# A graph network kernel on Trainium2: bias of the first merge from PSUM, and roots and shifts of the norms moved ahead

## The chip, the cores and the metric

One core of a Trainium2 chip runs the whole program. The metric is device microseconds of one execution.

## What is computed

The input is a graph of N = 3125 nodes with 256 features each (x) and E = 53125 edges (src, dst, sorted by dst, with loops). Four blocks follow each other; each is added to its input and normalised by row:

```python
x = _layernorm(x + _L0_gnn_ref(x, src, dst, ...))   # attention over edges, 8 heads, then out @ Wo.T + bo
x = _layernorm(x + _L1_gnn_ref(x, ..., src, dst))   # attention with additive scores, 4 heads
x = _layernorm(x + _L2_gnn_ref(x, src, dst, ...))   # 5 GIN layers with batch norm
x = _layernorm(x + _L3_gnn_ref(x, edge_index, ...)) # 3 SAGE layers

def _layernorm(x, axis=-1, eps=1e-05):
    m = jnp.mean(x, axis=axis, keepdims=True)
    v = jnp.var(x, axis=axis, keepdims=True)
    return (x - m) / jnp.sqrt(v + eps)
```

The change touches the sum x + bo of the first block, and all four layernorms.

## The kernel before, in words

The node rows stand in SBUF as x, 128 partitions by NT = 25 tiles of 256, and are handled in NSLAB = 5 slabs of SLAB = 5 tiles. The program is a sequence of phases (`Phase`), each with a block of instructions for every engine and a barrier of all engines at its end: prepare, edges and merge of the first block, norm 0, tables, edges and merge of the second block, norm 1, the GIN layers, norm 2, the SAGE layers, norm 3. Within a phase every engine has its own queue in the order in which the code is written, and waits on semaphores.

**The merge** (`merge_parts`, called for the first block with `biased=(x, bias_out)`). Sums over parts of edge groups are combined: TensorE turns 28 tiles of rows into three PSUM banks (L1370), VectorE scales them by an inverse (`make_rows`, L1415), POOL scatters each tile to the array out0 in memory with an indirect DMA (L1522). Meanwhile VectorE runs scans over the chunks; TensorE turns their result, ScalarE copies it, and POOL scatters it in four more indirect DMAs (L1530). POOL then waits until all are stored. The PSUM bank `side_ps` is read once at the start of this phase. At the end of its queue VectorE computes index columns (L1505, L1509) and adds the output bias, loaded as `bias_out` (a row of 256, the same on all partitions), to the five slabs of x (L1514), whose rows SyncE has loaded.

**The norm** (`residual_norm`). What is added comes in one of two ways. With `by_tile` (norms 0, 2 and 3) TensorE brings a tile at a time into a PSUM bank `in_ps`: for norm 0 it turns a tile of the loaded `more` (L1767), ScalarE copies it (`copy_more`, L1723), TensorE multiplies it by the weight w_out (L1776); for norms 2 and 3 it turns a tile of h_t (L1757). VectorE adds it to x (`add_tile`, L1651). In norm 1 a whole slab is added from SBUF (`add_slab`, L1661). Then VectorE takes the statistics of each tile (L1653), closes the slab (`close_slab`: aggregate L1668, variance plus epsilon into `std`, L1670), ScalarE takes the root (`root`, L1701), VectorE the reciprocal (L1676) and the shift, minus mean times reciprocal (`make_shift`, L1678), and ScalarE normalises each tile (`normalise`, L1706). In norms 0, 1 and 2 TensorE turns the normalised tile into `out_ps` (L1796) and ScalarE copies it (`copy_turned`, L1711). In norm 0 TensorE also makes the products alpha from it (L1804), which ScalarE copies by slab (L1716), SyncE stores, and POOL gathers into `alpha_parts` (L1641) as soon as the slabs that a gather needs are stored. In norm 3 SyncE stores the rows to the output (L1613).

Three orders matter for the change. On VectorE, the `by_tile` norms make the shift of a slab only after the first AHEAD = 2 tiles of the next slab are added, and norm 1 makes it ahead of the next slab:

```python
for s in range(NSLAB):
    if s and not by_tile:
        make_shift(s - 1)
    add_slab(s)
    for t in tiles(s):
        add_tile(t)
        if s and by_tile and t % SLAB == AHEAD - 1:
            make_shift(s - 1)
    close_slab(s)
```

On ScalarE, the root of a slab is the first instruction of that slab's turn, so it stands behind the copies that end the turn of the slab before (the last turned tiles; in norm 0 also two `copy_more`). On TensorE, the turns of normalised tiles and the bringing in of tiles AHEAD of the next slab alternate in a fixed order, which the change leaves alone.

Of the kernel before, what the change touches and what calls it, by code (L numbers as in the profile page):

```python
# [9 lines left out]
ALU = mybir.AluOpType  # L10
# [1281 lines left out]
def merge_parts(nc, keep, layer, out_rows, scale, loads=(), biased=None):  # L1292
# [5 lines left out]
    with Phase(nc) as ctx:  # L1298
# [112 lines left out]
        def _(v):  # L1411
# [91 lines left out]
            if biased:  # L1503
                to, of = biased
                nc.vector.tensor_copy(base[:, :], keep["part_node"][:, :]).then_inc(base_set, 1)  # L1505
                v.wait_ge(base_set, 1)
                for g in range(NSLAB):
                    of_slab = slice(CT + g * SLAB if g else 0, CT + (g + 1) * SLAB)
                    nc.vector.tensor_scalar(keep["alpha_index"][:, of_slab], base[:, of_slab], float(-g * SLAB * P), 0.0, ALU.add,  # L1509
                                            ALU.max).then_inc(apart_set, 1)  # L1510
                v.wait_ge(fetched, 16 * len(loads))
                for s in range(NSLAB):
                    slab = slice(s * SLAB, (s + 1) * SLAB)
                    nc.vector.tensor_tensor(to[:, slab, :], to[:, slab, :], of[:, :].unsqueeze(1).to_broadcast([P, SLAB, D]), ALU.add)  # L1514

        @block.gpsimd
        def _(pool):
# [25 lines left out]
def residual_norm(nc, keep, scratch, layer, add=None, added_t=None, turned_to=None, rows_to=None,  # L1543
# [8 lines left out]
    with Phase(nc) as ctx:  # L1552
# [93 lines left out]
        def _(v):  # L1646
# [25 lines left out]
            def make_shift(s):  # L1672

                slab = span(s)
                v.wait_ge(rooted, s + 1)
                nc.vector.reciprocal(std[:, slab], std[:, slab]).then_inc(inv, 1)  # L1676
                v.wait_ge(inv, s + 1)
                nc.vector.scalar_tensor_tensor(out=shift[:, slab], in0=mean_var[:, slab, 0], scalar=-1.0, in1=std[:, slab],  # L1678
                                               op0=ALU.mult, op1=ALU.mult).then_inc(shifted, 1)

            for s in range(NSLAB):
                if s and not by_tile:
                    make_shift(s - 1)
                add_slab(s)
                for t in tiles(s):
                    add_tile(t)
                    if s and by_tile and t % SLAB == AHEAD - 1:
                        make_shift(s - 1)
                close_slab(s)
            make_shift(NSLAB - 1)  # L1690
            if wide > D:
# [5 lines left out]
        def _(act):  # L1697
# [21 lines left out]
            def copy_more(t):  # L1719
                act.wait_ge(more_turned, t + 1)  # L1720
                if t >= 2:
                    act.wait_ge(in_turned, t - 1)
                nc.scalar.activation(more_t[:, t % 2, :, :], turn_ps[t % 2][:, 0:D].rearrange("p (k n) -> p k n", k=KH),  # L1723
                                     ACT.Copy).then_inc(more_copied, 1)

            if weight is not None:
                for t in range(SLAB + AHEAD):
                    copy_more(t)
            for s in range(NSLAB):
                root(s)  # L1730
                for t in tiles(s):
                    normalise(t)
                    if turned_to is not None and t % SLAB:
                        copy_turned(t - 1)
                    if alpha_to is not None and s and t % SLAB == 1:
                        copy_alpha(s - 1)
                    if weight is not None and t + SLAB + AHEAD < NT and t % SLAB < SLAB - AHEAD:
                        copy_more(t + SLAB + AHEAD)
                if turned_to is not None:
                    copy_turned(t)  # L1740
                if weight is not None and s + 2 < NSLAB:
                    for u in range(AHEAD):
                        copy_more((s + 2) * SLAB + u)
# [854 lines left out]
```

## Time and profile before

| what | value |
|---|---|
| median of 3 runs | 3120.46 us (3116.26 to 3121.49) |
| the profiled execution, its own time | 3124.26 us |
| its span, first to last instruction | 3122.5 us |
| mean granted TensorE clock | 0.930 of full speed |
| busy: TensorE, VectorE, ScalarE, POOL | 90%, 50%, 36%, 32% |
| first merge with its bias, until the first load of norm 0 | to 761.75 us |
| norm 0, norm 1 | about 762 to 832, 1493 to 1530 us |
| norm 2, norm 3 | about 2491 to 2531, 3087 to 3122 us |

Times in the trace are microseconds from the start of the span. A timeline row shows the start, the duration, the engine, the line, the operation with its output and inputs, how many instructions were merged into the row, and in brackets how long the engine was idle before and what ended that. Instructions on VectorE and ScalarE overlap a little with the next one, so the distance between starts is shorter than a duration.

### The profile page before, as it was taken

What the parts mean: (1) busy time and instruction counts of PE and PEld (TensorE: products, weight loads), DVE (VectorE), ACT (ScalarE), POOL (GpSimd) and SP (SyncE); (2) the same over time, 40 slices, a digit from 0 to 9 for tenths busy, and PEclk for the clock granted to TensorE, in tenths of its full rate; (3) what the DMA queues carried; (4) which work ended last, traced back from release to release, by engine and by line L of the source; (5) the groups of instructions that cost most, each with busy time, mean ns of one, the idle gap of its engine ahead of it and who ended that gap; (6) DMA issues with size and microseconds to landing.
All of it is one profiled execution on the core that took longest, in us unless ns stands there. A gap on an engine that the chain in (4) does not pass through costs nothing. (4 is left out here: it accounts for less than half of the span.)

```text
span 3122.5 us, 54367 instructions
## 1 busy us (share of the span) xinstructions
PE 2812.2 (90%) x17824; PEld 2045.7 (66%) x17824; DVE 1559.0 (50%) x2731; ACT 1117.4 (36%) x3112; POOL 988.6 (32%) x1020
## 2 busy tenths in 40 slices
PE   6789999994878999996599999999999879999997
PEld 4679999983668888985255555556555455565553
DVE  8689999975277878885412315133151340120203
ACT  6135555551446777772302204031040340110102
POOL 4477777745377777763000101001010000000000
PEclk7989999995878999997699999999999989999998
DMA  6799999953248989992343341424324034233321
GB/s 232 234 316 317 316 319 317 314 197 120 43 111 140 144 153 148 157 144 59 120 156 102 110 130 53 160 78 136 129 68 132 1 134 139 84 129 129 105 96 41
DMA packets 327372, 469.35 MB, mean 150 GB/s; under 512 B 154903, under 2 KB 237927, under 8 KB 326453
## 3 DMA queue, kind: packets, MB, share of 16 engines
q1 hardware_dynamic: 264228, 285.42, 33.6%
q0 software_dynamic: 59088, 176.67, 18.7%
q10 hardware_dynamic: 3776, 3.80, 0.4%
q8 instruction: 144, 2.36, 0.3%
q14 instruction: 136, 1.11, 0.1%
HBM read 412.09 MB, written 55.44 MB: 150 GB/s over the span
## 5 line engine op out<-in xcount | busy, mean ns | idle before, releaser
L1138 ACT ACTIVATE sums<-e_part_ps 128x384 f32 x832 | 413.6, 497 | 402.3 <-PE e_part_ps L1036 287.0
L2014 PE MATMUL gin_sum_ps<-slab,high 128*128 128x391 f16 x2000 | 499.3, 331 | 1.9 <-DMA slab<-adj 1.5
L2014 PE MATMUL gin_sum_ps<-slab,low 128*128 128x391 f16 x2000 | 499.2, 331 | 0.0
L846 POOL DMA_INDIRECT e_from_src<-val,src x416 | 393.3, 946 | 157.5 <-issue 98.5
L846 POOL DMA_INDIRECT e_from_src<-vk,src x416 | 393.4, 946 | 142.5 <-issue 105.7
L2361 PE MATMUL sage_sum_ps<-slab,high 128*128 128x391 f16 x1200 | 298.6, 330 | 7.2 <-DVE low L2443 4.1
L1034 PE MATMUL e_part_ps<-e_onehot,e_from_src 128*128 128x129 f32 x1664 | 286.1, 296 | 14.4 <-ACT ends L1140 7.7
L2361 PE MATMUL sage_sum_ps<-slab,low 128*128 128x391 f16 x1200 | 298.4, 330 | 0.0
L2191 DVE SCALAR_TENSOR_TENSOR z_t<-h_t,gin_own,gin_sum_ps 128x391 f32<-128x391 f32 x80 | 44.8, 618 | 490.1 <-PE gin_sum_ps L2014 490.1
L2076 POOL TENSOR_SCALAR h_t<-h_t 128x391 f32<-128x391 f32 x32 | 40.6, 1279 | 783.3 <-DVE h_t L2221 783.3
L2014 PEld LDWEIGHTS gin_sum_ps<-slab,low 128*128 128x128 f16 x2000 | 195.5, 98 | 140.5 <-issue 3.6
L914 DVE TENSOR_TENSOR e_from_src<-e_from_src,e_fixed 128x2048 f32<-128x2048 f32 x104 | 237.5, 2284 | 87.8 <-ACT e_fixed L1119 86.4
L2014 PEld LDWEIGHTS gin_sum_ps<-slab,high 128*128 128x128 f16 x2000 | 195.3, 98 | 130.6 <-issue 4.1
L1034 PE MATMUL e_part_ps<-x,e_from_src 128*128 128x129 f32 x1664 | 268.7, 284 | 3.0 <-DVE e_from_src L914 2.3
L2085 ACT ACTIVATE gin_y_t<-gin_proj_ps,gin_columns 128x391 f32<-128x391 f32 x80 | 46.8, 585 | 572.6 <-PE gin_proj_ps L2027 572.6
L1034 PEld LDWEIGHTS e_part_ps<-e_onehot,e_from_src 128*128 128x128 f32 x1664 | 228.1, 199 | 32.1 <-ACT ends L1140 17.9
L1034 PEld LDWEIGHTS e_part_ps<-x,e_from_src 128*128 128x128 f32 x1664 | 231.0, 192 | 22.1 <-DVE e_from_src L914 4.0
L1004 PE MATMUL e_spread_ps<-e_window,x 128*128 128x256 f32 x832 | 216.1, 387 | 14.8 <-DMA e_window<-q_part 13.7
L2449 DVE TENSOR_TENSOR z_t<-sage_sum_ps,sage_inv_degree_all 128x391 f32<-128x391 f32 x48 | 24.0, 558 | 352.7 <-PE sage_sum_ps L2361 352.7
L2418 ACT ACTIVATE h_t<-sage_proj_ps,sage_columns 128x391 f32<-128x391 f32 x48 | 25.6, 584 | 412.3 <-PE sage_proj_ps L2376 412.3
L2361 PEld LDWEIGHTS sage_sum_ps<-slab,high 128*128 128x128 f16 x1200 | 116.6, 98 | 84.9 <-DVE low L2443 5.9
L2361 PEld LDWEIGHTS sage_sum_ps<-slab,low 128*128 128x128 f16 x1200 | 117.0, 98 | 83.6 <-issue 1.0
(325 smaller groups left out, 4824.7 us busy)
## 6 DMA issues: line engine op xcount, KB each, us to landing
slab<-adj SPq DMA_DIRECT2D x160, 977.5 KB, 4.8
e_window<-q_part SPq DMA_DIRECT2D x416, 128.0 KB
adj<-e_counts SPq DMA_DIRECT2D x8, 1250.0 KB
adj<-e_counts SPq DMA_DIRECT2D x8, 1193.8 KB
e_from_src<-vk,src POOLq DMA_INDIRECT x416
e_from_src<-val,src POOLq DMA_INDIRECT x416
e_window<-alpha_part SPq DMA_DIRECT2D x416, 4.0 KB
vk<-pr_kv_out SPq DMA_DIRECT2D x25, 256.0 KB, 4.1
```

Of the source, the lines that this page charges most:

```text
L846: nc.gpsimd.indirect_dma_start(from_src[:, b, j, :], None, by_src, bass.IndirectOffsetOnAxis(ap=keep["src"][:, g * G + j:g * G + j + 1], a ...
L914: nc.vector.tensor_tensor(from_src[:, b, :, 0:D].rearrange("p j (h d) -> p j h d", h=H), from_src[:, b, :, 0:D].rearrange("p j (h d) -> p ...
L1004: mm = nc.tensor.matmul(to, onehot_t[:, r, j, :], window[:, r, j, :], start=True, stop=True)
L1034: nc.tensor.matmul(part_ps[s][:, k * ENDS:(k + 1) * ENDS], from_src[:, b, j, k * P:(k + 1) * P], onehot[:, b, j, :], start=True, stop=True)
L1138: nc.scalar.activation(keep["sums"][:, :, bass.ds(starts[j], P)], of[:, :, 0:P], ACT.Copy).then_inc(whole_copied, 1)
L2014: mm = nc.tensor.matmul(sum_ps[KH * n + m][:, 0:AN], part[:, t, m * P:(m + 1) * P], slab[:, s, n, k * AN:(k + 1) * AN], start=(t == 0 and ...
L2076: nc.gpsimd.tensor_scalar(h_t[:, 1, cols(b)], h_t[:, 1, cols(b)], 0.0, None, ALU.max).then_inc(floored, 1)
L2085: nc.scalar.activation((z_t if p else y_t)[:, m, cols(b)], proj_ps[v % (2 * KH)][:, 0:AN], ACT.Identity, bias=columns[:, 3 * p, m:m + 1], ...
L2191: nc.vector.scalar_tensor_tensor(out=z_t[:, m, cols(b)], in0=h_t[:, m, cols(b)], scalar=own[:, l:l + 1], in1=sum_ps[KH * n + m][:, 0:AN], ...
L2361: mm = nc.tensor.matmul(sum_ps[KH * n + m][:, 0:AN], part[:, t, m * P:(m + 1) * P], slab[:, s, n, k * AN:(k + 1) * AN], start=(t == 0 and ...
L2418: nc.scalar.activation(h_t[:, m, cols(b)], proj_ps[v % (2 * KH)][:, 0:AN], ACT.Relu if l + 1 < LAYERS else ACT.Identity, bias=columns[:, m ...
L2449: nc.vector.tensor_tensor(z_t[:, m, cols(b)], sum_ps[KH * n + m][:, 0:AN], inv_degree[:, cols(b)], ALU.mult).then_inc(evacuated, 1)
```

## The change

The bias row is first copied to the free PSUM bank `side_ps`, and the five adds read it there. In the `by_tile` norms the shift of a slab is made ahead of the next slab's first tile, as in norm 1. On ScalarE the root of slab s + 1 is issued right after the last normalise of slab s, ahead of the copies that follow it; the root of slab 0 stands alone in front. No instruction is added except the one copy.

```diff
                 v.wait_ge(fetched, 16 * len(loads))
+                nc.vector.tensor_copy(side_ps[:, 0:D], of[:, :]).then_inc(base_set, 1)
+                v.wait_ge(base_set, 2)
                 for s in range(NSLAB):
                     slab = slice(s * SLAB, (s + 1) * SLAB)
-                    nc.vector.tensor_tensor(to[:, slab, :], to[:, slab, :], of[:, :].unsqueeze(1).to_broadcast([P, SLAB, D]), ALU.add)
+                    nc.vector.tensor_tensor(to[:, slab, :], to[:, slab, :],
+                                            side_ps[:, 0:D].unsqueeze(1).to_broadcast([P, SLAB, D]), ALU.add)
...
             for s in range(NSLAB):
-                if s and not by_tile:
+                if s:
                     make_shift(s - 1)
                 add_slab(s)
                 for t in tiles(s):
                     add_tile(t)
-                    if s and by_tile and t % SLAB == AHEAD - 1:
-                        make_shift(s - 1)
                 close_slab(s)
...
+            root(0)
             for s in range(NSLAB):
-                root(s)
                 for t in tiles(s):
                     normalise(t)
+                    if t % SLAB == SLAB - 1 and s + 1 < NSLAB:
+                        root(s + 1)
                     if turned_to is not None and t % SLAB:
                         copy_turned(t - 1)
```

How the queues read, by the program's order (lines in the changed kernel are up to 3 higher). VectorE in norm 0, from the end of one slab into the next, before:

```order
L1668 BN_AGGR n_mean_var<-n_stats 128x2 x5
L1670 TENSOR_SCALAR n_std<-n_mean_var 128x5
L1651 TENSOR_TENSOR x<-x,n_in_ps 128x256
L1653 BN_STATS n_stats<-x 128x6
L1651 TENSOR_TENSOR x<-x,n_in_ps 128x256
L1653 BN_STATS n_stats<-x 128x6
L1676 RECIPROCAL n_std<-n_std 128x5
L1678 SCALAR_TENSOR_TENSOR n_shift<-n_mean_var,n_std 128x5
L1651 TENSOR_TENSOR x<-x,n_in_ps 128x256
L1653 BN_STATS n_stats<-x 128x6
```

The same place of VectorE's queue in the changed kernel:

```order
L1671 BN_AGGR n_mean_var<-n_stats 128x2 x5
L1673 TENSOR_SCALAR n_std<-n_mean_var 128x5
L1679 RECIPROCAL n_std<-n_std 128x5
L1681 SCALAR_TENSOR_TENSOR n_shift<-n_mean_var,n_std 128x5
L1654 TENSOR_TENSOR x<-x,n_in_ps 128x256
L1656 BN_STATS n_stats<-x 128x6
L1654 TENSOR_TENSOR x<-x,n_in_ps 128x256
L1656 BN_STATS n_stats<-x 128x6
```

The reciprocal and the shift moved past two tiles, so they now directly follow the variance (n_std) on which the root between them depends. ScalarE in norm 0, from the last but one normalise of a slab to the first of the next, before:

```order
L1706 ACTIVATE x<-x,n_shift,n_std 128x256
L1711 ACTIVATE x_t<-n_out_ps 128x2x128
L1706 ACTIVATE x<-x,n_shift,n_std 128x256
L1711 ACTIVATE x_t<-n_out_ps 128x2x128 x2
L1723 ACTIVATE n_more_t<-n_turn_ps 128x256 x2
L1701 ACTIVATE n_std<-n_std 128x5
L1706 ACTIVATE x<-x,n_shift,n_std 128x256
```

The same place of ScalarE's queue in the changed kernel:

```order
L1707 ACTIVATE x<-x,n_shift,n_std 128x256
L1712 ACTIVATE x_t<-n_out_ps 128x2x128
L1707 ACTIVATE x<-x,n_shift,n_std 128x256
L1702 ACTIVATE n_std<-n_std 128x5
L1712 ACTIVATE x_t<-n_out_ps 128x2x128 x2
L1724 ACTIVATE n_more_t<-n_turn_ps 128x256 x2
L1707 ACTIVATE x<-x,n_shift,n_std 128x256
```

The root moved ahead of two copies of turned tiles and two copies of input tiles; in norms 1 and 2 the last two don't exist, and in norm 3 none of the four.

## Rows read from the trace of the kernel before

**Rows 1.** The page, busy time of the engines (us, share, instructions).
```profile
PE 2812.2 (90%) x17824; PEld 2045.7 (66%) x17824; DVE 1559.0 (50%) x2731; ACT 1117.4 (36%) x3112; POOL 988.6 (32%) x1020
```
**Rows 2.** Timeline of POOL, end of the first merge (start, duration, operation, idle before).
```profile
737.63 7.70 POOL L1522 DMA_INDIRECT out<-m_rows,part_index  x1 [0.30 <-issue]
745.64 0.98 POOL L1522 DMA_INDIRECT out<-m_rows,part_index  x1 [0.30 <-issue]
...
755.94 0.89 POOL L1530 DMA_INDIRECT out<-m_chunk_rows,chunk_index  x1 [0.30 <-issue]
```
**Rows 3.** Timeline of VectorE and SyncE, end of the first merge.
```profile
737.38 7.09 DVE L1514 TENSOR_TENSOR x<-x,bias_out 128x1280 f32<-128x1280 f32 x5
...
761.75 3.94 SPq L1607 DMA_DIRECT2D n_more<-out  x5
```
**Rows 4.** Timelines of ScalarE, VectorE and TensorE in norm 0, before slab 2.
```profile
795.98 0.39 ACT L1711 ACTIVATE x_t<-n_out_ps 128x256 f32<-128x256 f32 x1 [0.83 <-PE n_out_ps L1796]
...
797.62 0.20 ACT L1701 ACTIVATE n_std<-n_std 128x5 f32<-128x5 f32 x1
800.76 0.60 ACT L1706 ACTIVATE x<-x,n_shift,n_std 128x256 f32<-128x256 f32 x1 [2.95 <-DVE n_shift L1678]
...
796.76 0.17 DVE L1670 TENSOR_SCALAR n_std<-n_mean_var 128x5 f32<-128x5 f32 x1
798.47 0.42 DVE L1651 TENSOR_TENSOR x<-x,n_in_ps 128x256 f32<-128x256 f32 x1 [1.54 <-PE n_in_ps L1776]
...
796.41 0.61 PE L1804 MATMUL n_alpha_ps<-w_alpha,x_t 128*128 128x8 f32 x4
...
801.41 0.44 PE L1796 MATMUL n_out_ps<-ident,x 128*128 128x128 f32 x2 [1.89 <-ACT x L1706]
```
**Rows 5.** Timelines of ScalarE and VectorE in norm 2, before slab 1.
```profile
2502.93 0.39 ACT L1711 ACTIVATE h_t<-n_out_ps 128x256 f32<-128x256 f32 x1
...
2505.96 1.09 ACT L1706 ACTIVATE x<-x,n_shift,n_std 128x256 f32<-128x256 f32 x2 [1.65 <-DVE n_shift L1678]
...
2503.90 0.17 DVE L1670 TENSOR_SCALAR n_std<-n_mean_var 128x5 f32<-128x5 f32 x1
```
**Rows 6.** Timelines of VectorE and ScalarE in norm 3, slabs 3 and 4.
```profile
3106.77 0.17 DVE L1670 TENSOR_SCALAR n_std<-n_mean_var 128x5 f32<-128x5 f32 x1
3106.85 0.41 DVE L1651 TENSOR_TENSOR x<-x,n_in_ps 128x256 f32<-128x256 f32 x1
...
3111.67 0.17 DVE L1670 TENSOR_SCALAR n_std<-n_mean_var 128x5 f32<-128x5 f32 x1
3112.11 0.19 DVE L1676 RECIPROCAL n_std<-n_std 128x5 f32<-128x5 f32 x1 [0.27 <-ACT n_std L1701]
...
3112.54 2.56 ACT L1706 ACTIVATE x<-x,n_shift,n_std 128x256 f32<-128x256 f32 x5 [0.46 <-DVE n_shift L1678]
```
**Rows 7.** Groups by line and shape, VectorE (busy us, mean ns, idle before).
```profile
L852 DVE COPY e_fixed<-iota 128x128 f32<-128x128 f32 x2 | 0.6, 294 | 31.5 <-PEq L74 31.5
```
**Rows 8.** Timelines of VectorE and POOL in the first block's edge phase.
```profile
179.87 2.28 DVE L914 TENSOR_TENSOR e_from_src<-e_from_src,e_fixed 128x2048 f32<-128x2048 f32 x1
...
181.32 0.95 POOL L846 DMA_INDIRECT e_from_src<-vk,src  x1 [0.30 <-issue]
```
**Rows 9.** All instructions of line 846, first block: ns min/median/max.
```profile
L846 POOL DMA_INDIRECT e_from_src<-vk,src x416: 940/946/955, 146.3 to 666.0; - x139
```
**Rows 10.** Timeline of POOL, second merge.
```profile
1478.19 0.98 POOL L1522 DMA_INDIRECT out<-m_rows,part_index  x1 [0.30 <-issue]
```
**Rows 11.** Timelines of ScalarE (slab 0) and POOL (gathers) in norm 0.
```profile
775.95 1.28 ACT L1701 ACT_TABLE_LOAD   x1
...
819.88 0.94 POOL L1641 DMA_INDIRECT alpha_parts<-alpha,alpha_index  x1 [6.57 <-DMA alpha<-n_alpha]
```
**Rows 12.** Timeline of ScalarE in norm 1, before slab 1.
```profile
1506.92 0.20 ACT L1701 ACTIVATE n_std<-n_std 128x5 f32<-128x5 f32 x1
1507.58 1.09 ACT L1706 ACTIVATE x<-x,n_shift,n_std 128x256 f32<-128x256 f32 x2 [0.46 <-DVE n_shift L1678]
```

## The prediction

> **What bounds the kernel now.** I read the page first: TensorE is busy for 90% of the span [rows 1]. But the change touches none of the stages in which that work lies. It touches the end of the first merge and the four residual norms, short stages between barriers, so what counts is which engine ends each of them. For that I read the timeline of each engine there.
>
> First merge. POOL scatters the merged rows to memory by indirect DMAs, one every 1.29 us: from 745.64 to 755.94 there are eight such steps [rows 2]. One of them, issued at 737.63, takes 7.70 us instead of 0.98 [rows 2]. In the same time, from 737.38 to 744.47, VectorE adds the bias to x in five instructions [rows 3]. POOL resumes 0.9 us after the last of them, which is what one issue takes. ScalarE and TensorE are long done, VectorE ends at 744.47, and the next stage's first load comes at 761.75 [rows 3], 4.92 us after POOL's last issue ends (755.94 + 0.89). So POOL ends this stage and the long issue is on the path.
>
> Norms. ScalarE's first normalising instruction of a slab waits for the slab's shift. In norm 0 the variance of slab 2 is there at 796.76, and the normalise starts at 800.76, 4.00 us later, having waited 2.95 us [rows 4]. In norm 2 the distance is 2.06 us (2503.90 to 2505.96) [rows 5]. The last slab, which has no next tiles ahead of its shift, shows the direct way: variance 3111.67, reciprocal 3112.11, normalise 3112.54, so 0.87 us [rows 6]. In norm 3 there is nothing behind ScalarE to win: VectorE runs without a gap and ends the stage (the add of rows 6 that starts 0.08 us after the variance).
>
> **The bias.** The change adds a copy of 128x256 into PSUM and one wait. The nearest row is a copy of 128x128 at 294 ns [rows 7]; with twice the columns I take 0.45 us. The five adds have the same size, so VectorE ends near 744.9, while POOL, freed, would end at 756.83 - 6.72 = 750.11: 5 us of cover. If POOL were not freed, both would simply slip: +0.45. The question is whether an add with one operand in PSUM leaves POOL alone. The trace has that form: the edge phase's 2.28 us product reads and writes e_from_src in SBUF and takes its second operand from the PSUM tile e_fixed. Inside one such instruction (179.87 to 182.15) POOL issues at 181.32 in 0.95 us [rows 8], and the longest of 416 issues in that phase is 955 ns [rows 9], though 52 of these products run beside them. Nor is it the number of DMAs outstanding: the second merge, with the same scatters and no bias, shows 0.98 after its last row is made [rows 10]. Term: 7.70 - 0.98 = **-6.7**; ends +0.45 and -7.0.
> The Trainium skill ("SBUF — State Buffer", section "Who interferes with whom") says that a tensor_tensor with both inputs in SBUF contends only with POOL instructions that read SBUF, and infers that descriptor generation is not among what it stops. By that the 7.70 would have another cause and the sum would be 6.7 us smaller; rows 2 and 3 speak against it here, since the issue ends with the adds. Indirect issues read their index column from SBUF, which the first half of the rule would cover.
>
> **Norm 0** (TensorE is the busy engine in it). Two moves. (a) On VectorE the shift goes ahead of the next slab's first two tiles, whose projections TensorE makes only after ScalarE's copies: the add at 798.47 had waited 1.54 us for them [rows 4]. (b) On ScalarE the root goes ahead of two copies of turned tiles and two copies of input tiles. Slab 2 worked out: ScalarE ends the last normalise of the slab before at about 795.15, stands until the variance is out (796.76 + 0.17), roots (0.20) until 797.15. The first copy that started at 795.98 [rows 4] now starts near 797.1, **1.1 later**; the shift is out at 797.6, the four copies take until about 798.7, and the normalise can start there, 2.0 earlier than 800.76. But TensorE's alpha product (796.41 [rows 4]) waits for the held copy and also comes 1.1 later, and behind it the same 3.0 us of work for two tiles (796.41 to 799.4) has to be done before the next turn: 797.53 + 3.0 = 800.5 instead of 801.41 [rows 4]. So **0.9** per slab, for slabs 1 to 3. Slab 0: the table load ends at 777.23 [rows 11], then root, reciprocal and shift give a normalise at 777.9 instead of 776.73 + 2.06 = 778.79: 0.85. Slab 4: nothing, it was direct. Together 3.5 on TensorE. The stage, though, is ended by POOL's ten gathers from 819.88 on, the first of which waited 6.57 us for slab 2's alpha store [rows 11]. That store comes 3.5 earlier; the five gathers of slab 3 then wait for their own store some 1 us, since its slab's shift gains nothing. Term: **-2.5**; ends 0 and -4.5 (no such wait, and the held copies costing nothing).
>
> **Norm 1** (no tiles are brought in; its order on VectorE is unchanged, only the root moves). ScalarE's root stood behind the copy of the last turned tile, at 1506.92; the normalise followed at 1507.58 [rows 12]. Now the shift is out before that copy, and the normalise can start behind it where the root did: 0.66 saved at each of four slabs, **-2.6**; ends -1.5 and -3. Per slab VectorE then needs 4.5 us and ScalarE 4.95, so ScalarE is next.
>
> **Norm 2.** Variance 2503.90, root from 2504.10, shift out at 2504.7. Two copies of turned tiles, the first at 2502.93 before [rows 5], now stand behind the root and end the normalise's wait at about 2504.85: 1.1 earlier than 2505.96. The two tiles then added behind the shift take 1.6 us on VectorE, and the third needs TensorE's next turn 1.8 after the normalise, so they stay hidden. Slabs 0 to 3 gain, slab 4 doesn't: 4 x 1.15 = **-4.6**; ends -3.5 and -5.
>
> **Norm 3, a cost.** VectorE is the bound. Before, variance to next add took 0.08 (3106.77 to 3106.85 [rows 6]) and the shift of the slab 0.29 later on: 0.37. Now VectorE stands for the root: variance to reciprocal 0.44 [rows 6], reciprocal to the next add about 0.31: 0.75. Four slabs at 0.38: **+1.5**, all on the last normalise and the last store; ends 0 and +2.
>
> **Sum.** -6.7 - 2.5 - 2.6 - 4.6 + 1.5 = -14.9. Against the profiled execution's own 3124.26 that is 3109.4; that execution lies 3.8 above the median of the runs shown, so against the median of 3120.46 it is **3105.5**. All stages lie between barriers, so nothing starts early that could take the gain back; but each later stage meets TensorE's clock at another moment, for which I allow 2 us either way.
>
> **The rivals.**
> 1. POOL isn't freed. For it: the row that shows an unhindered issue is a gather, not a scatter. Against: the stall begins and ends with the adds. The norms alone give -8.2, the copy +0.45: 3112.7. Chance 0.07. (By the inference of the Trainium skill's SBUF page quoted above, this would be the outcome.)
> 2. Slower than before. ScalarE stands at each root before copies that TensorE and VectorE need, and the delay is handed round: 1.1 x 4 in norm 0, 1.3 x 4 in norm 2 (2502.93 to about 2504.2), 0.2 x 4 in norm 1, 1.5 in norm 3: +11.9, less 6.7 for the bias, +5.2: 3125.7. It decides where a held copy costs more than the early shift returns (2.0 in norm 0, 1.15 in norm 2). Against: TensorE waited 1.89 us for ScalarE's normalise at the next step anyway [rows 4], so the delay has room. Chance 0.04.
> 3. Only norm 0 gives nothing, because its held copies cost what the shift gains: 3108. Chance 0.15.
> The upper ends of the norm terms (-4.5, -3, -5, 0) with the bias give 3101.3; that is part of the forecast.
>
> **How the numbers follow.** About 0.2% (6 us) is what a measurement of this kernel tells from no change. Forecast with its variations 0.74, rivals 0.07, 0.04 and 0.15. Faster by over 0.2% is under 3114.2: the forecast, rival 3 and most of rival 1, 0.93; within 0.2%: the rest of rival 1 and most of rival 2, 0.05; slower 0.02. The range goes from the upper ends (3101.3, with one of the 2 us for the clock) to rival 1: 3100 to 3112.5.
>
> **What would show it.** Right: every scatter of the first merge at about 1 us, and the load of norm 0 some 6.7 us earlier; the variance-to-normalise distance 0.9 to 2.0 us in all slabs; norm 1's slab period 4.95 instead of 5.6, norm 2's 5.8 instead of 7.0, norm 3's 5.3 instead of 4.9. Wrong: a scatter of over 5 us beside the adds; TensorE idle before the alpha product in norm 0 for longer than the wait at 801.41 has shrunk; a last store of norm 3 that doesn't move by VectorE's four stalls.

## The result, and the profile after

| | before | changed |
|---|---|---|
| median of 4 runs each | 3120.95 us (3116.26 to 3121.49) | 3100.49 us (3093.94 to 3102.35) |
| profiled execution, its span | 3124.26, 3122.5 us | 3101.5, 3099.7 us |
| mean granted TensorE clock | 0.930 | 0.932 |

The ratio is 0.9949, with a 95% interval of 0.9929 to 0.997: the changed kernel is 20.5 us faster, at the low end of the predicted range (3100 to 3112.5) and 5 us below the predicted 3105.5. Measured again beside 18 runs of the kernel before it stood at 0.9946 (0.9933 to 0.9958).

The page's first line, against [rows 1]: POOL is busy 6.6 us less, about what its one long issue had in excess. TensorE and ScalarE, with the same instructions, differ by 3.3 and 2.1 us; the rest of the gain is waiting that went away.
```profile
PE 2808.9 (91%) x17824; PEld 2042.4 (66%) x17824; DVE 1561.0 (50%) x2732; ACT 1115.3 (36%) x3112; POOL 982.0 (32%) x1020
```
**First merge.** Timelines of POOL, VectorE and SyncE at its end, against [rows 2, 3].
```profile
740.54 0.98 POOL L1525 DMA_INDIRECT out<-m_rows,part_index  x1 [0.30 <-issue]
741.83 0.98 POOL L1525 DMA_INDIRECT out<-m_rows,part_index  x1 [0.30 <-issue]
...
750.85 0.89 POOL L1533 DMA_INDIRECT out<-m_chunk_rows,chunk_index  x1 [0.30 <-issue]
...
740.18 0.42 DVE L1512 COPY m_side_ps<-bias_out 128x256 f32<-128x256 f32 x1
740.63 7.08 DVE L1516 TENSOR_TENSOR x<-x,m_side_ps 128x1280 f32<-128x1280 f32 x5
...
756.66 4.08 SPq L1610 DMA_DIRECT2D n_more<-out  x5
```
The adds take as long as before (7.08 against 7.09 us), but scatters now pass beside them in 0.98 us. From the first scatter of the merge to the start of the last it was 51.89 us (704.05 to 755.94) and is 45.18 (705.67 to 750.85): **-6.7 us**.

**Norm 0.** Timelines of ScalarE, VectorE and TensorE around the root of slab 2, against [rows 4].
```profile
788.37 0.21 ACT L1702 ACTIVATE n_std<-n_std 128x5 f32<-128x5 f32 x1 [1.81 <-DVE n_std L1673]
788.48 0.64 ACT L1712 ACTIVATE x_t<-n_out_ps 128x256 f32<-128x256 f32 x2
...
790.10 0.59 ACT L1707 ACTIVATE x<-x,n_shift,n_std 128x256 f32<-128x256 f32 x1
...
788.16 0.17 DVE L1673 TENSOR_SCALAR n_std<-n_mean_var 128x5 f32<-128x5 f32 x1
788.83 0.16 DVE L1681 SCALAR_TENSOR_TENSOR n_shift<-n_mean_var,n_std 128x5 f32<-128x5 f32 x1
...
788.90 0.61 PE L1807 MATMUL n_alpha_ps<-w_alpha,x_t 128*128 128x8 f32 x4 [0.93 <-ACT x_t L1712]
...
791.57 0.38 PE L1799 MATMUL n_out_ps<-ident,x 128*128 128x128 f32 x2
```
Variance to normalise is 1.94 us (788.16 to 790.10) instead of 4.00. The price is here too: ScalarE stands 1.81 us before the root with two copies behind it, and TensorE's alpha product waits 0.93 us for the first of them. Behind it TensorE has 2.67 us of work (788.90 to 791.57) up to its next turn.

**Norms 1, 2 and 3.** First norm 1's ScalarE, slab 1 [rows 12]; then ScalarE and VectorE of norm 2 [rows 5]; then VectorE of norm 3, slab 1, and ScalarE, slab 4 [rows 6].
```profile
1490.80 0.21 ACT L1702 ACTIVATE n_std<-n_std 128x5 f32<-128x5 f32 x1
1491.90 1.08 ACT L1707 ACTIVATE x<-x,n_shift,n_std 128x256 f32<-128x256 f32 x2
...
2485.08 0.21 ACT L1702 ACTIVATE n_std<-n_std 128x5 f32<-128x5 f32 x1 [1.16 <-DVE n_std L1673]
2485.74 1.09 ACT L1707 ACTIVATE x<-x,n_shift,n_std 128x256 f32<-128x256 f32 x2
...
2484.87 0.17 DVE L1673 TENSOR_SCALAR n_std<-n_mean_var 128x5 f32<-128x5 f32 x1
...
3073.20 0.17 DVE L1673 TENSOR_SCALAR n_std<-n_mean_var 128x5 f32<-128x5 f32 x1
3073.64 0.19 DVE L1679 RECIPROCAL n_std<-n_std 128x5 f32<-128x5 f32 x1 [0.27 <-ACT n_std L1702]
3073.94 0.41 DVE L1654 TENSOR_TENSOR x<-x,n_in_ps 128x256 f32<-128x256 f32 x1
...
3089.85 2.56 ACT L1707 ACTIVATE x<-x,n_shift,n_std 128x256 f32<-128x256 f32 x5 [0.46 <-DVE n_shift L1681]
```
In norm 2 the normalise comes 0.87 us behind the variance (2.06 before). In norm 3 VectorE stands 0.74 us from the variance to its next add (3073.20 to 3073.94; 0.08 before).

By stage, each measured between the same two instructions in both traces (us):

| stage | before | changed | difference | predicted |
|---|---|---|---|---|
| first merge, first to last scatter | 51.89 | 45.18 | -6.7 | -6.7 |
| norm 0, load to the tables' first product | 74.60 | 67.12 | -7.5 | -2.5 |
| norm 1, load to the next stage's first product | 38.98 | 36.51 | -2.5 | -2.6 |
| norm 2, first product to the next stage's | 39.66 | 34.02 | -5.6 | -4.6 |
| norm 3, first add to last slab's first normalise | 24.97 | 26.44 | +1.5 | +1.5 |
| sum | | | -20.8 | -14.9 |

The spans differ by 22.8 us. The other 2 us lie in stages with the same instructions, which differ between any two profiles: from the tables of norm 0 to the load of norm 1 it is 656.7 us before and 654.1 in the changed kernel, and between 651.1 and 660.5 in the kernels below. What was left to find out was why norm 0 gave three times its term, which of the two moves gives what, and whether the PSUM operand is what freed POOL.

### The profile page after: what moved, and what is told of

Read it like the earlier page. It is cut to its first block and busy times, and to the rows that moved or that the text cites. A ratio compares the mean times of both kernels' runs of the same rounds, so it can differ in the third digit from the quotient of the medians.

```text
span 3099.7 us, 54368 instructions
## 1 busy us (share of the span) xinstructions
PE 2808.9 (91%) x17824; PEld 2042.4 (66%) x17824; DVE 1561.0 (50%) x2732; ACT 1115.3 (36%) x3112; POOL 982.0 (32%) x1020
```

## The experiments

### The change in parts

**Only the bias.** The changed kernel's merge with the norms of the kernel before:
```diff
+                nc.vector.tensor_copy(side_ps[:, 0:D], of[:, :]).then_inc(base_set, 1)
+                v.wait_ge(base_set, 2)
...
-                    nc.vector.tensor_tensor(..., of[:, :].unsqueeze(1).to_broadcast([P, SLAB, D]), ALU.add)
+                    nc.vector.tensor_tensor(..., side_ps[:, 0:D].unsqueeze(1).to_broadcast([P, SLAB, D]), ALU.add)
```


> Only the bias goes through PSUM; the norms stay as before. My theory: the scatter of 7.70 us becomes 0.98, so from the first scatter of the first merge to POOL's last issue 46.1 us instead of 52.8, and the norms keep their periods (11.35 in norm 0, 5.61 in norm 1, 6.97 in norm 2, 4.89 in norm 3): 6.7 us less, with up to 2 us for TensorE's clock in norm 0. Rival: part of the large gain in norm 0 came from its earlier start (TensorE's clock), not from the order; then norm 0 alone would be 2 to 4 us shorter here than the 74.6 us (load to tables) of before, though its order is untouched.

Measured: 3116.76 us, ratio 0.9987 (0.9976 to 0.9998) against 23 runs of the kernel before, so 0.6 to 7.5 us faster than the 3120.08 of these. The trace sizes the part better than the median does: no scatter beside the adds over 0.99 us, and 46.1 us from the first scatter's start to the last issue's end where it was 52.8, so 6.7 us. Norm 0 took 74.7 us, as before, with 11.36 us from the first normalise of slab 1 to that of slab 2: POOL's earlier end alone changes nothing there.

**Only the norms.** The changed kernel with the old adds (bias read from SBUF, no copy).

> Only the order in the norms is changed; the bias is added from SBUF as before. My theory: the 7.70 us scatter is back, norm 0 has slab periods of about 10.05 instead of 11.35, norm 1 4.95, norm 2 5.3 to 5.8, norm 3 5.26: 2.2 to 3.5 + 4 x 1.3 in norm 0, 2.6 in norm 1, 5 in norm 2, less 1.5 in norm 3, so 11 to 14 us less than before. Rival (the clock in norm 0 follows from the stage's earlier start): norm 0 gains under 5 us here and the whole under 11.

Measured: 3106.85 us, ratio 0.9952 (0.9938 to 0.9967). The long scatter is back (7.68 us). Norm 0 took 70.3 us, norm 2 34.1 us. The whole is 13.2 us below the 3120.08 us of the kernel before, inside the 11 to 14 expected; norm 0's share, 4.3 us, lies under the 5 us that the rival named, and the second run of the changed kernel, below, says why. The intervals of this and of the whole change overlap, so the medians don't resolve the 6.7 us; the length of the merge does (52.8 and 46.1 us).

**Only the shift ahead.** The root goes back behind the copies:
```diff
-            root(0)
             for s in range(NSLAB):
+                root(s)
                 for t in tiles(s):
                     normalise(t)
-                    if t % SLAB == SLAB - 1 and s + 1 < NSLAB:
-                        root(s + 1)
```


> The changed kernel with the root back where it stood, behind the copies; the shift stays ahead of the tiles. My theory: in norm 0 the root now holds no copy back, TensorE's alpha product is not late and the period falls to about 9.4 (TensorE without a gap), 3 x 0.7 less than in the changed kernel; norm 1 is back at 5.61 (+2.6); norm 2 as in the changed kernel; so within 1 us of it, 18 to 21 us less than before. Rival: the root's place matters more than the shift's; then norm 0 loses most of its gain and the kernel is over 5 us slower than the changed one.

**Only the root ahead.** The shift goes back behind two tiles of the next slab in norms 0, 2 and 3:
```diff
-                if s:
+                if s and (not by_tile):
                     make_shift(s - 1)
                 add_slab(s)
                 for t in tiles(s):
                     add_tile(t)
+                    if s and not (not by_tile) and t % SLAB == AHEAD - 1:
+                        make_shift(s - 1)
```


> The changed kernel with the shift back behind the next slab's two tiles; the root stays ahead of the copies. My theory: in norm 0 the root holds the copies by 1.1 us, and the shift still waits for the two tiles that need them, so the period is 12.4 instead of 11.35 (+1.1 at four slabs); norm 1 keeps its 2.6; norm 2 and 3 as before. Sum with the bias -6.7 + 4.4 - 2.6 = -5 against before. Rival: the root's place alone brings the gain; then norm 0 and 2 are as short as in the changed kernel, some 15 us less than before.

Measured: shift alone 3104.38 us, ratio 0.9947 (0.9931 to 0.9963); root alone 3118.58 us, ratio 0.9998 (0.9986 to 1.0009), both with the new bias. So in time the shift carries all of the norms' gain, and the root on balance none. The root alone missed its expectation of 5 us less: the median is 1.5 us less (interval 4.4 less to 2.8 more), though its merge and norm 1 are shorter by 6.7 and 2.6 us. The traces say what each move does, norm by norm (us; a middle slab is the distance from the first normalise of a slab to that of the next):

| | root, shift | norm 0, a middle slab | norm 0 in all | norm 1 | norm 2 | norm 3 |
|---|---|---|---|---|---|---|
| only the bias | late, late | 11.36 | 74.7 | 39.3 | 39.7 | 25.0 |
| only the root | early, late | 12.17 | 75.6 | 36.4 | 39.5 | 25.0 |
| only the shift | late, early | 9.25 | 65.5 | 39.2 | 34.1 | 26.4 |
| changed | early, early | 10.05 | 67.1 | 36.5 | 34.0 | 26.4 |

The middle slabs, all with TensorE at its upper clock level, show the order alone: the parts add up. The column for the whole of norm 0 holds TensorE's clock too: while tiles were still being brought in it fell for a stretch twice with only the bias and never in the other three, and after the wait for the load it rose between 3.5 and 6.4 us after the first matmul. The early shift is worth 2.1 us a slab in norm 0 and 5.6 us in norm 2, and costs 1.5 in norm 3. The early root gives norm 1 its gain of 2.6 to 2.9 us and **costs norm 0 0.8 us a slab**. Norm 0, slab 2, with the shift alone (ScalarE, VectorE):
```profile
783.78 0.38 ACT L1712 ACTIVATE x_t<-n_out_ps 128x256 f32<-128x256 f32 x1 [0.24 <-PE n_out_ps L1797]
784.06 0.84 ACT L1724 ACTIVATE n_more_t<-n_turn_ps 128x256 f32<-128x256 f32 x2
784.80 0.20 ACT L1702 ACTIVATE n_std<-n_std 128x5 f32<-128x5 f32 x1
785.45 0.60 ACT L1707 ACTIVATE x<-x,n_shift,n_std 128x256 f32<-128x256 f32 x1 [0.46 <-DVE n_shift L1681]
...
783.95 0.17 DVE L1673 TENSOR_SCALAR n_std<-n_mean_var 128x5 f32<-128x5 f32 x1
```
ScalarE does its copies while the variance is still being made and isn't idle before the root. The normalise follows 1.50 us behind the variance, sooner than the 1.94 us of the changed kernel, where the held copies stand between root and normalise.

### Norm 0 again, and a version that takes the better order of each norm

The changed kernel was measured a second time.

> The changed kernel once more, as the base line of this call. Theory (the gain of norm 0 holds two parts: 4.9 us that the order of the work gives and about 2.6 us that TensorE's clock gave in the one profiled execution, 1.3 for a rise one step earlier and 1.3 for a low stretch that was absent): load of norm 0 to first matmul of the tables between 67.1 us (no low stretch, early rise) and about 69.7 (one of each), with the normalise periods of the second and third slab at 10.05 us wherever the clock stays up; the periods of norm 1 4.95, norm 2 5.77 and 5.26, norm 3 5.26. Rival (the change itself keeps the clock up): 67.1 again, no low stretch. Time about 3101 us, 0.5 per cent below the kernel before.

The first stretch of TensorE in norm 0, in three kernels: the kernel before, the changed kernel as first profiled, and the changed kernel again.
```profile
766.15 1.11 PE L1767 MATMUL n_turn_ps<-ident,n_more 128*128 128x128 f32 x4 [28.01 <-DMA n_more<-out]
767.31 2.07 PE L1776 MATMUL n_in_ps<-w_out,n_more_t 128*128 128x256 f32 x4
769.60 1.91 PE L1776 MATMUL n_in_ps<-w_out,n_more_t 128*128 128x256 f32 x4
771.73 1.40 PE L1776 MATMUL n_in_ps<-w_out,n_more_t 128*128 128x256 f32 x4
```
```profile
761.12 1.12 PE L1770 MATMUL n_turn_ps<-ident,n_more 128*128 128x128 f32 x4 [20.21 <-DMA n_more<-out]
762.28 2.07 PE L1779 MATMUL n_in_ps<-w_out,n_more_t 128*128 128x256 f32 x4
764.57 1.06 PE L1779 MATMUL n_in_ps<-w_out,n_more_t 128*128 128x256 f32 x4
```
```profile
762.15 1.11 PE L1770 MATMUL n_turn_ps<-ident,n_more 128*128 128x128 f32 x4 [20.20 <-DMA n_more<-out]
763.31 2.07 PE L1779 MATMUL n_in_ps<-w_out,n_more_t 128*128 128x256 f32 x4
765.61 1.91 PE L1779 MATMUL n_in_ps<-w_out,n_more_t 128*128 128x256 f32 x4
767.74 1.35 PE L1779 MATMUL n_in_ps<-w_out,n_more_t 128*128 128x256 f32 x4
...
781.94 1.81 PE L1779 MATMUL n_in_ps<-w_out,n_more_t 128*128 128x256 f32 x4
783.97 1.76 PE L1779 MATMUL n_in_ps<-w_out,n_more_t 128*128 128x256 f32 x4
786.01 1.03 PE L1779 MATMUL n_in_ps<-w_out,n_more_t 128*128 128x256 f32 x4
```
Four products of a tile's projection take about 2 us at the lower level of the clock (1.2 GHz) and 1.03 at the upper (2.4 GHz). After the wait for the load TensorE starts at the lower one. It reached the upper one 6.4 us after its first matmul in the kernel before, 3.7 in the changed kernel and 6.3 in the same kernel again, after the same idle time of 20.2 us. The second profile also has a low stretch in the middle (781.94 to 785.6), with a slab of 11.73 us instead of 10.05, as the kernel before had one (one such group took 1.75 us from 813.26). So the second profile meets the clock as the kernel before did, and its norm 0 took 70.23 us. Like compared with like, the order of the work gives 74.60 - 70.23 = **4.4 us**, and 3.1 of the 7.5 us were the clock. The low stretches weren't quite alike: from slab 3's normalise to slab 4's variance the kernel before took 8.45 us, and the kernel with only the root ahead 7.13 at full clock, so there the stretch cost about 1.3 us and not 1.7. The order's part is thus 4.4 to 4.8 us. The expectation for this run, 69.7 us for such a profile, was half a microsecond too low, since I had priced the low stretch at 1.3 us, and it cost 1.7. Of the nine profiles with this order in norm 0 (the kernels of the next part among them), seven took 69.6 to 70.3 us and two (with the rise after 3.7 and 3.2 us, and no low stretch) 67.1 and 66.9. The rival, that the change itself keeps the clock up, is out: seven of the nine have the low stretch. The second run's median was 3102.81 us, ratio 0.9946 (0.9933 to 0.9958).

**Norm 3 as before**, all else changed (the shift of norm 3 behind two tiles).

> The changed kernel, but norm 3 alone takes its shift behind two tiles of the next slab again. Theory (norm 3's own order costs it 0.37 us a slab and 1.5 us in all, since its adds and not TensorE set its pace): periods of norm 3 back at 4.89 us with 3.7 for the last, from its first add to its last slab's normalise 24.97 instead of 26.44, so 1.5 us less than the changed kernel, about 3099.5 us. Rival (the last slab's work behind norm 3 takes back what the slabs gain): periods 4.89, time of the changed kernel.

Its norm 3 went back to 4.89 us a slab, with 3.7 for the last, and 24.95 us from first add to last normalise instead of 26.4: the mechanism is as expected. The time isn't: median 3107.45 (3095.45 to 3114.53, 7 runs), ratio 0.9967 (0.9954 to 0.9979), 4.6 us above the changed kernel beside it, where 1.5 below was expected. The profiled execution was the fastest of the seven, with a span of 3093.7 us, so its trace can't show where the others spent more; that stays open.

**The best of each norm**: shift ahead in norms 0 to 2, root behind the copies in norm 0, norm 3 as before.
```diff
-                if s:
+                if s and (turned_to is not None):
                     make_shift(s - 1)
...
+                    if s and not (turned_to is not None) and t % SLAB == AHEAD - 1:
+                        make_shift(s - 1)
...
-            root(0)
+            if (weight is None):
+                root(0)
             for s in range(NSLAB):
+                if not (weight is None):
+                    root(s)
                 for t in tiles(s):
                     normalise(t)
-                    if t % SLAB == SLAB - 1 and s + 1 < NSLAB:
+                    if (weight is None) and t % SLAB == SLAB - 1 and s + 1 < NSLAB:
                         root(s + 1)
```


> Each norm in the order that the single parts favour: norm 0 with the shift ahead but the root behind the copies, norms 1 and 2 as changed, norm 3 with the shift behind two tiles. Theory (parts add up, and the early root costs norm 0 0.8 us a slab while it gives 0.8 us once): norm 0 65.5 us from load to tables with slab periods of 9.25 us instead of 10.05; norm 1 4.95, norm 2 5.77 and 5.26, norm 3 4.89; 1.6 + 1.5 = 3.1 us below the changed kernel, about 3098 us. Rival (norm 0's end is set by its gathers, so its slabs' gain is lost there): norm 0 67 us, only 1.5 us below the changed kernel.

Measured: 3099.12 us (3098.28 to 3100.1, 5 runs), ratio 0.9936 (0.9924 to 0.9949), against 3102.81 (3100.18 to 3104.54) of the changed kernel on the same chip: 3.7 us less, with 3.1 expected, and each of its five runs below each of the other's. By trace: norm 0 66.65 us (65.5 expected), its slabs 9.25, with the clock's late rise; norm 1 4.95, norm 2 5.26 to 5.78, norm 3 4.89 us a slab. The rival was not wholly wrong. POOL, gathers of norm 0:
```profile
813.50 0.94 POOL L1644 DMA_INDIRECT alpha_parts<-alpha,alpha_index  x1 [0.85 <-DMA alpha<-n_alpha]
```
Here the gathers of slab 3 do wait for their store: the stop I had predicted for the changed kernel, where the ten gathers ran without one. The fast slabs alone don't bring it, since the kernel with only the shift ahead has the same order in norm 0, slabs of 9.25 us and no stop. But in the best kernel TensorE ran at the lower level in slab 4 (four alpha products took 0.86 us from 809.48 on, 0.51 at the upper), and ScalarE's copy of slab 3's alphas came 7.59 us behind slab 2's instead of 6.93.

### What holds a scatter

> The changed kernel, but the bias add of slabs 0 and 1 reads the bias from SBUF and only slabs 2 to 4 from PSUM. Theory (an add with both inputs in SBUF holds a scatter's issue for as long as it runs): one scatter of about 3.5 to 3.8 us (two adds of 1.42 us and 0.9 behind them), the others 0.98 or a little above, and the 40 scatters take 46.1 + 2.7 = 48.8 us. Rival A (a scatter is held by what VectorE has queued, until it is idle): one scatter of about 7.7 us, 52.8 us in all. Rival B (it was the wait on the fetched bias and not the operand): all 0.98, 46.1 us.

The adds of slabs 0 and 1 read SBUF, all behind the copy. POOL and VectorE:
```profile
741.05 0.98 POOL L1525 DMA_INDIRECT out<-m_rows,part_index  x1 [0.30 <-issue]
742.34 1.15 POOL L1525 DMA_INDIRECT out<-m_rows,part_index  x1 [0.30 <-issue]
743.79 1.10 POOL L1525 DMA_INDIRECT out<-m_rows,part_index  x1 [0.30 <-issue]
...
741.14 2.89 DVE L1516 TENSOR_TENSOR x<-x,bias_out 128x1280 f32<-128x1280 f32 x2
743.95 4.27 DVE L1516 TENSOR_TENSOR x<-x,m_side_ps 128x1280 f32<-128x1280 f32 x3
```
(The merge has 32 scatters, not the 40 that this and the next expectations say; the times given for them are meant from the first one's start to the last one's end, and stand.) None of the three expectations held. The scatter that starts at 742.34, beside the first add, ends at 743.49, which is 0.86 us behind that add's end (742.63) and in the middle of the second add from SBUF. It waited for one add, not for the two that read SBUF. (This kernel's median, 3110.42 us, is 7.6 above the changed kernel's for 0.3 us more in the merge; in its profile the stretch from the tables of norm 0 to the load of norm 1, unchanged, took 660.5 us against 652.9 beside it.) Four more kernels, one run each, moved the adds against the scatters and changed their number.

> The changed kernel with its copy of the bias to PSUM kept and unused, and all five bias adds reading it from SBUF: the same instructions at the same times as in the mixed kernel, where two adds from SBUF held one scatter by 0.17 us and one by 0.11. Theory A (a scatter that starts in the last tenths of an add is let in at that add's end, whatever follows; the long hold of the kernel before needs a scatter that asks early in an add): no scatter over about 1.3 us, 46.1 to 46.6 us for the 40. Theory B (the run of adds behind decides: five in a row from SBUF shut scatters out to their end, two don't): one scatter of about 6.6 us that ends 0.86 us behind the last add, about 51.7 us for the 40.

> The changed kernel, but the adds of slabs 0 and 1 read the bias from SBUF and come ahead of the copy to PSUM, and those of slabs 2 to 4 read PSUM: the two adds stand where the first two of the kernel before stood, with a scatter that starts 0.25 us into the first. Theory A (a scatter that asks early in an add from SBUF waits out the whole run of them): one scatter of 3.5 us (from 0.25 us into two adds of 2.88 us, and 0.86 behind them), 48.6 us for the 40. Theory B (the hold depends on how many such adds follow): no scatter over 2.2 us, at most 47.3 us.

> The kernel with five bias adds from SBUF and two copies of the bias to PSUM ahead of them, unused, so that the adds start about 0.8 us later against the scatters and a scatter starts some 0.7 us into the first add. Theory P (where in the first add the scatter asks decides: at 0.25 us it waits out the run of adds, as in the kernel before; from 0.36 us on only the add that runs): one scatter of about 1.6 us, 47.2 us or less for the 40. Theory N (how many such adds are in the queue when it asks in the first add decides): one scatter of about 7.2 us, 52.3 us for the 40.

> The changed kernel, but the adds of slabs 0 to 3 read the bias from SBUF and come ahead of the copy to PSUM, and that of slab 4 reads PSUM. Theory N (with more such adds in a row the scatter isn't let in between them): one scatter held to the end of the fourth add, 6.2 us, 51.4 us for the 40. Theory P: 6.2 us if the scatter starts about 0.25 us into the first add, about 2.0 us and 47.2 us for the 40 if it starts at 0.36 us or later.

POOL and VectorE of the four, in that order (five adds behind the copy; two adds ahead of it; five behind two copies; four ahead of it):
```profile
734.39 0.59 DVE L1429 TENSOR_TENSOR m_own<-ends,m_wide_ps 128x416 f32<-128x416 f32 x1 [1.09 <-PE m_wide_ps L1378]
...
740.69 1.16 POOL L1525 DMA_INDIRECT out<-m_rows,part_index  x1 [0.30 <-issue]
742.15 1.10 POOL L1525 DMA_INDIRECT out<-m_rows,part_index  x1 [0.30 <-issue]
...
739.50 7.10 DVE L1516 TENSOR_TENSOR x<-x,bias_out 128x1280 f32<-128x1280 f32 x5
```
```profile
741.65 1.98 POOL L1526 DMA_INDIRECT out<-m_rows,part_index  x1 [0.30 <-issue]
...
741.28 2.88 DVE L1517 TENSOR_TENSOR x<-x,bias_out 128x1280 f32<-128x1280 f32 x2
```
```profile
740.63 1.48 POOL L1526 DMA_INDIRECT out<-m_rows,part_index  x1 [0.30 <-issue]
...
739.76 7.10 DVE L1517 TENSOR_TENSOR x<-x,bias_out 128x1280 f32<-128x1280 f32 x5
```
```profile
738.75 6.18 POOL L1526 DMA_INDIRECT out<-m_rows,part_index  x1 [0.30 <-issue]
...
738.39 5.69 DVE L1517 TENSOR_TENSOR x<-x,bias_out 128x1280 f32<-128x1280 f32 x4
```
Their times, one run each, are 3107.21, 3106.36, 3103.37 and 3114.03 us beside 3114.24, 3114.24, 3111.47 and 3111.47 of the kernel before; single runs don't size such a part, the length of the merge does. Seven kernels with adds from SBUF now stand side by side (two and three is the mixed kernel above):

| kernel | adds from SBUF | scatter starts in the first add after | held until the end of | merge, 32 scatters |
|---|---|---|---|---|
| before | 5 | 0.25 us | the fifth add | 52.8 |
| only the norms | 5 | 0.27 | the fifth | 52.8 |
| four first | 4 | 0.37 | the fourth | 51.3 |
| two first | 2 | 0.36 | the first | 47.2 |
| five, mid | 5 | 0.87 | the first | 47.0 |
| five, late | 5 | 1.19 | the first | 46.7 |
| two and three | 2 | 1.20 | the first | 46.4 |
| changed | none | | not held | 46.1 |

In all seven the held scatter ends 0.86 us behind the end of an add, so its end is tied to that of an add. How long it is held depends on two things. Late in the first add it is let in at that add's end, though four more are to come. Early in it, it waits for the last of four or five, but for the first only of two (0.37 us with four against 0.36 with two). Theory P held for five adds at 0.87 us and theory N for four at 0.37, and neither alone gives the table. A rule that gives both isn't settled, with one trace a row.

For the change this means that the PSUM operand wasn't needed for most of the gain. The kernel with five late adds has the changed kernel's copy and its times, and differs in the operand alone. It holds five scatters by 0.11 to 0.18 us each, 0.6 us in all, and the changed kernel none: that is what the operand is shown to give. The other 6.1 of the 6.7 us (52.8 to 46.7) come from where the adds stand against the scatters. They start 34.96 us after the merge's first scatter, where in the kernel before it was 33.33: 0.46 us is the copy, and 1.17 comes with a wait of VectorE ahead of it for four products of TensorE (the first line shown for the four kernels), which took 3.14 us at the lower clock level, as here and in the changed kernel, and 2.03 us in the kernel before, where the clock rose among them. The wait by itself doesn't free the scatter, since the kernel with four adds ahead of the copy has it too and holds one for 6.18 us; with the copy ahead of the adds there is no long hold.

What a PSUM operand does to a scatter that starts early in an add, where the long holds were, no run shows: beside the adds from PSUM none started less than 0.57 us into one. The nearest rows are in the edge phase of the kernel before, where gathers that start 0.03 to 0.35 us into a product with its second operand in PSUM take 0.94 or 0.95 us, as all do.

## Why the prediction was right or wrong

- **What bounds the stages**: right. No engine does less, and every gain is a wait in the stages between barriers that the prediction named.
- **The bias, -6.7**: right in size, and the scatters beside the adds are 0.98 us, the copy 0.42 us (0.45 taken). The reason given, that an operand in PSUM leaves POOL alone, agrees with every scatter beside such an add, but alone it is shown for 0.6 us. The other 6.1 came with the later start of the adds, which the prediction didn't weigh: that the same kernel with the bias left in SBUF would have had them too makes the term's size partly luck. The reason implied for the 7.70 us, that adds with both inputs in SBUF shut a scatter out for as long as they run, was too broad: five such adds that start at another point against the scatters cost 0.6 us. Rival 1 (not freed) is out. The rule of the Trainium skill quoted there ("SBUF — State Buffer", "Who interferes with whom") infers that such adds don't stop descriptor generation; in seven kernels here they hold the issue, each time with an end 0.86 us behind an add. Whether it is the reading of the index column from SBUF or the generation that stops, no run tells. Of VectorE's 2-port modes, which it says tensor_tensor doesn't have, the Trainium skill says in the same section that whoever issues first gets the shared pair for the whole instruction. The holds here were like that in four kernels of the table, with a release at the end of one add; in three the hold went over four or five instructions.
- **Norm 0, -2.5**: the mechanism was right, the term too small. At about the same behaviour of the clock it measures -4.4 to -4.8. The step on slab 0 (0.85) measured 0.86 (load to normalise 17.04 us, and 16.18 in the second profile). "Behind it the same 3.0 us of work" was the step that failed for slabs 1 to 3: it was 2.67 us (788.90 to 791.57). Of the 5.00 us between alpha product and next turn [rows 4] that leaves 5.00 - 2.67 - 1.03 for the later start = 1.3 a slab, where 0.9 was predicted; the slab periods, 11.36 and 10.05, say the same. "The five gathers of slab 3 then wait some 1 us" failed too: they didn't wait. Another 2.7 to 3.1 us of the first profile were TensorE's clock, for which the prediction had allowed 2 us in all; the kernel's second profile took them back.
- **Held copies**: the 1.1 us by which they were to start later is 1.03 us at the alpha product, counted from the slab's first turn, and the root alone showed their cost by itself, 0.8 us a slab in norm 0. Rival 2 had this cost but gave it no return: in norm 0 the shift returns 2.1 a slab, so it never decided. Rival 3 (norm 0 gives nothing) is out, though it named the right mechanism, and that is real: with the root late, norm 0 is 1.6 us shorter (65.5 and 67.1 us) although the clock rose later there, and by its slabs 3 x 0.8 = 2.4.
- **Norm 1, -2.6**: right, 4.95 us a slab as worked out, from the root alone.
- **Norm 2, -4.6**: measured -5.6 in the first profile and -5.6 in the second. Predicted was 1.15 a slab and a period of 5.8. The variance-to-normalise distance fell by 1.19 (2.06 to 0.87), but the periods are 5.77, 5.26, 5.68 and 5.27 us in turn, and the granted clock goes with them:
```profile
2479.97:2485.74 5.77, 4.58 (x20) 3.78 (x20) 4.96 (x19) 4.33 (x12) 0.00 (x0) 0.57 0.00 0
2485.74:2491.00 5.26, 3.12 (x20) 2.09 (x20) 4.71 (x19) 4.15 (x13) 0.00 (x0) 1.00 0.00 2
```
(start and end, length, busy time of TensorE, its weight loads, VectorE, ScalarE and POOL, then the clock: 0.57 and 1.00.) The predicted 5.8 is the slab with the clock low; the two slabs at full clock give the further 1.0 us, for which norm 2's term had nothing (the sum allowed 2 us either way for the clock as a whole). The gain comes from the shift alone (39.7 to 34.1); the root's move, which the prediction took as half of the mechanism there, is worth 0.1.
- **Norm 3, +1.5**: right in size and place, 5.26 us a slab and 0.74 us from variance to next add.
- **The sum**: -14.9 predicted; -20.8 by stages in the first profile, some -17.7 to -18.1 with norm 0 at the clock of the kernel before. The 3 us that are left are norm 0 and norm 2. The changed kernel's two medians, 3100.49 and 3102.81, are 5.0 and 2.7 below the predicted 3105.5. That the first is still inside the range owes something to its width: part of it was the clock, and part two terms that were too small.

## What to carry to other kernels

An early root or shift is worth what it frees minus what it holds on the engine's queue, so decide it for each stage by the engine that bounds it: the same move gave 2.6 to 2.9 us in one norm and took 0.8 a slab in another. Where an indirect DMA's issue is long beside VectorE work, look at where in the VectorE instruction it starts as well as at the operand, and separate the two: a kernel with the copy made and unused showed that most of the gain wasn't the operand's. And before a difference in a short stage is put down to the order of the work, compare the durations of one repeated matmul group in both traces: here about 3 of 7.5 us were the clock.

## What the runs showed of the hardware

- A scatter's issue (0.98 us alone) beside adds of 1.49 us with both inputs in SBUF was held by 0.1 to 6.7 us, depending on how far into an add it started and on how many adds stood in a row; with the second input in PSUM it never was, at starts 0.57 us or more into an add.
- TensorE's clock, after 20 us of waiting and more, rose 3.2 to 6.4 us after the first matmul of norm 0, in two profiles of one kernel 3.7 and 6.3 us after it, and a low stretch within norm 0's slabs, while tiles were still being brought in, came in nine of fourteen profiles. They are worth about 1.3 and 1.3 to 1.7 us, as much as some terms of the change.
- The same instructions between norm 0 and norm 1 took 651.1 to 660.5 us in the profiles. Two versions within 2 us of the changed kernel in their short stages had medians 4.6 and 7.6 us above it, and the traces don't show why.
